# Router and latent projections: weights' high and low parts side by side in one moving operand

## The chip, the cores and the metric

The kernel runs on one core of a Trainium2 chip. The metric is the device time of one launch in microseconds (us). Before the change it is 628.88 us (median of three runs, 627.64 to 630.49). All inputs, weights and outputs are in float32 in HBM.

The engines are named as in the profile: PE is TensorE, PEld its loads of stationary operands, DVE VectorE, ACT ScalarE, POOL GpSimd and SP the engine that issues most DMAs.

## The reference

One transformer layer over 8 batches of 256 tokens of width 256: attention with compressed keys and values, then a mixture of experts. Only what the change touches is spelled out; rotary embedding, the routed experts and the shared expert are as usual.

```python
x = x + attention(layernorm(x))
#   kv = x_hat @ Wkv_a                     # [256 tokens, 64 latents + 64 rotary], per batch
#   kv_c = layernorm(kv[:, :64]) * gamma + beta;   k_rope = rope(kv[:, 64:])
#   k, v from kv_c @ Wkv_b;  16 heads of softmax(q k^T) v, then @ Wout
x = x + moe(layernorm(x))
#   logits = x_hat @ gate_w                # [256 tokens, 8 experts], per batch
#   scores = softmax(logits); the two best experts of each token, weighted by their scores
#   plus a shared expert for all tokens
```

## The kernel before

**Three products for one.** PE multiplies in the type float32r, which keeps fewer bits than float32. So each operand is kept as a high part (rounded) and a low part (what is left), and a product is the sum of three: high times high, high times low, low times high. The helper `three` (L222) issues them into one PSUM accumulation. Each is a load of a stationary operand and a matmul that streams the moving one.

**The two stages that change.** Each batch has two tiles j of 128 tokens and two halves k of the width.
- The latents, `prep_kv` (L250, PE): the normalised input `xa` is stationary, `Wkv_a` (`wkva_hi`, `wkva_lo`, 128 columns each) moves. Two tiles, two halves, three products: twelve matmuls of 128 columns. VectorE then takes mean and variance of the 64 latents from PSUM (`prep_kv`, DVE), the rotary products (`prep_rot`) and, a round later, the normalised latents (`prep_kn`), all from PSUM.
- The logits, `logits(b)` (PE): `xf` is stationary, `gate_w` (`gw_hi`, `gw_lo`, 8 columns) moves: again twelve matmuls. VectorE takes the maximum (`gate_max`, L1484), ScalarE the exponentials (`gate_exp`, L1288), both from PSUM.

**The order of the work.** All five engines run lists written out by hand, with semaphores between them. Attention is 64 rounds g, one for each pair of heads: i = g // 8 is the batch, r = g % 8 the round in it. In every round PE does two heads' scores (`ps_s`), four turns of probabilities (`ps_t<-ident,probs`), a query product (`ps_q`, twelve matmuls for pair g + 4), the turn of the norms (`ps_o<-ident,rinv`), the output projection (`ps_y`) and the products with the values (`ps_o`). Beside it the lists have work for other batches:
- at r = 2 and 3 the turn and the latents of batch i + 1; at r = 4 and 5 VectorE's and GpSimd's work on them
- at r = 6 and 7 the turn and the logits of batch i - 1 (from PE's first half of the round, ahead of the query product); at r = 0 and 1 of the next batch VectorE's masks and PE's ranks
- at r = 6 and 7 of batches 0 to 4 (and at 6 of batch 5) the split of one part of the expert weights: ScalarE makes its high part (`mgu_hi`, L469), VectorE the low one (`mgu_lo`, L477)

The last batch's logits stand behind attention, between products of the shared expert. Batch 6's come in round 62.

**The query buffer.** `ps_q` is one buffer. Of each query product ScalarE copies two pieces (`swap`, `qswap<-ps_q`), VectorE then multiplies it by the cosines (`query_cos`, `qf<-ps_q,qcos`, L1434, first in its list of the next round), and PE's next query product waits for that.

In round r = 7 ScalarE's list reads: copy of the norms (`norm<-ps_o`), high part of the weights, `gate_exp`, `swap`. VectorE's reads: low parts of the probabilities, low part of the weights, `gate_max`, the second maximum of the scores, and in the next round `query_cos`:

```python
if g in part_round: split_lo(part_round[g])          # DVE, order in a round
...
if routed(i, r) == 7 and batch(i - 1): gate_max(i - 1)
```

The front (until 50 us) makes the combined head weights, and holds the latents of batch 0; its 16 heads have lists of their own.

## Time and profile before

| what | us |
|---|---|
| median of three runs | 628.88 |
| the profiled execution, its own time | 629.82 |
| its span | 628.1 |
| PE busy | 605.3 |
| DVE busy | 467.8 |
| ACT busy | 475.0 |
| POOL busy | 410.2 |

PE is busy for 96% of the span. Its matmuls are pipelined: one lasts about 0.28 us, and the next starts 0.11 or 0.12 us behind it, so a busy PE need not be at its peak, and the length of a stage is read from the starts of its first matmul and of the first behind it. A row of a timeline begins with the start in us from the span's start and the length in us; in brackets stands the idle time before it and who ended it. The names read output<-inputs, for a matmul output<-moving,stationary.

### The profile page before, as it was taken

To read this page: it belongs to the slowest core of one execution; us is meant where nothing else is said; L and a number is where in the kernel's file an instruction comes from. 1 tells how busy PE (TensorE), PEld (TensorE's weight loads), DVE (VectorE), ACT (ScalarE), POOL (GpSimd) and SP (SyncE) were. 2 spreads that over 40 slices of the span, in tenths; PEclk is the share of its full clock that TensorE was granted. 3 is DMA by queue.
4 is the path that set the end of the run, shared out by engine and by line. 5 is a ranking of instruction groups with operands and counts; after the bars stand their busy time and mean duration, and the time that the engine had idled before them with its cause. 6 is when DMAs were issued, how large, how long until landed. Compare 5 with 4: busy or idle time off the path is not lost. (4 is left out here: it accounts for less than half of the span.)

```text
span 628.1 us, 15730 instructions
## 1 busy us (share of the span) xinstructions
PE 605.3 (96%) x4916; PEld 591.3 (94%) x4916; DVE 467.8 (74%) x1406; ACT 475.0 (76%) x1331; POOL 410.2 (65%) x455
## 2 busy tenths in 40 slices
PE   8998999999999999999999999999979989999995
PEld 8888999999999999999999999999978979999994
DVE  6667786877886878788688887778666676666486
ACT  4779999898988989889898898979864335556531
POOL 1467897786897889789789978978613204444400
PEclk9998999999999999999999999999999889999998
DMA  9792000000001001000100100020603155444292
GB/s 259 238 345 41 2 1 3 2 1 35 11 10 43 11 18 43 10 19 3 43 18 10 43 9 19 9 78 11 184 2 118 51 173 166 124 132 120 86 320 83
DMA packets 34024, 45.41 MB, mean 72 GB/s; under 512 B 4056, under 2 KB 29112, under 8 KB 33944
## 3 DMA queue, kind: packets, MB, share of 16 engines
q1 hardware_dynamic: 29160, 34.56, 17.6%
q0 software_dynamic: 3408, 9.34, 4.6%
q8 instruction: 42, 0.69, 0.5%
q10 hardware_dynamic: 1376, 0.50, 0.3%
q14 instruction: 38, 0.31, 0.2%
HBM read 27.57 MB, written 16.82 MB: 71 GB/s over the span
## 5 line engine op out<-in xcount | busy, mean ns | idle before, releaser
L1245 ACT ACTIVATE probs<-ps_s,nmax 128x256 f32<-128x256 f32 x256 | 119.1, 477 | 10.8 <-DVE nmax L1439 10.7
L1785 POOL TENSOR_TENSOR qswap<-qswap,qsin 128x512 f32<-128x512 f32 x64 | 83.3, 1301 | 43.6 <-ACT qswap L1222 43.6
L226 PE MATMUL ps_q<-xa,wq_hi 128*128 128x256 f32 x512 | 101.0, 295 | 3.7 <-DVE qf L1434 3.7
L1439 DVE TENSOR_REDUCE nmax<-ps_s 128x2 f32<-128x512 f32 x128 | 86.8, 678 | 9.3 <-PE ps_s L226 8.6
L1222 ACT ACTIVATE pT_hi<-ps_t 128x512 fp32r<-128x512 f32 x128 | 76.7, 599 | 17.0 <-PE ps_t L978 15.6
L1788 POOL TENSOR_TENSOR qf<-qf,qswap 128x512 f32<-128x512 f32 x64 | 82.7, 1292 | 10.5 <-DVE qf L1434 6.5
L1792 POOL TENSOR_TENSOR q_lo<-qf,q_hi 128x512 fp32r<-128x512 f32 x64 | 82.9, 1296 | 5.8 <-ACT q_hi L1222 5.8
L226 PEld LDWEIGHTS ps_q<-xa,wq_hi 128*128 128x128 f32 x512 | 79.9, 192 | 5.5 <-DVE qf L1434 3.3
L299 DVE TENSOR_TENSOR pT_lo<-ps_t,pT_hi 128x512 fp32r<-128x512 f32 x128 | 81.9, 681 | 1.5 <-ACT pT_hi L1222 1.5
L226 PE MATMUL ps_o<-pT_hi,kv_hi 128*128 128x256 f32 x256 | 76.7, 300 | 2.5 <-ACT norm L1222 2.5
L226 PE MATMUL ps_s<-kT_hi,q_hi 128*128 128x256 f32 x256 | 77.6, 303 | 0.9 <-ACT probs L1245 0.9
L978 PE MATMUL ps_t<-ident,probs 128*128 128x128 f32 x512 | 76.8, 273 | 1.3 <-DVE pT_lo L299 1.3
L1222 ACT ACTIVATE qswap<-ps_q 32x512 f32<-32x512 f32 x128 | 75.6, 590 | 3.3 <-PE ps_q L226 1.0
L1813 POOL DMA_INDIRECT routed_out<-yb,to x39 | 37.4, 959 | 57.7 <-DVE to L1574 55.1
L226 PE MATMUL ps_q<-xa,wq_lo 128*128 128x256 f32 x256 | 73.0, 285 | 0.0
L226 PE MATMUL ps_s<-kT_hi,q_lo 128*128 128x256 f32 x256 | 71.9, 281 | 0.0
L226 PE MATMUL ps_s<-kT_lo,q_hi 128*128 128x256 f32 x256 | 71.8, 280 | 0.0
L226 PE MATMUL ps_o<-pT_hi,kv_lo 128*128 128x256 f32 x256 | 71.5, 279 | 0.0
L226 PE MATMUL ps_o<-pT_lo,kv_hi 128*128 128x256 f32 x256 | 71.4, 279 | 0.0
L978 PEld LDWEIGHTS ps_t<-ident,probs 128*128 128x128 f32 x512 | 59.4, 141 | 1.7 <-issue 1.7
L1796 POOL TENSOR_TENSOR o_lo<-on,o_hi 128x256 fp32r<-128x256 f32 x64 | 47.3, 739 | 17.9 <-ACT o_hi L1222 17.5
L1434 DVE TENSOR_TENSOR qf<-ps_q,qcos 128x512 f32<-128x512 f32 x64 | 43.7, 683 | 15.8 <-ACT qswap L1222 15.6
(337 smaller groups left out, 1914.5 us busy)
## 6 DMA issues: line engine op xcount, KB each, us to landing
xg<-routed_in SPq DMA_DIRECT2D x39, 129.0 KB, 2.2
normal_turned<-xf SPq DMA_DIRECT2D x8, 512.0 KB, 2.8
wq_raw<-Wq_dram SPq DMA_DIRECT2D x16, 192.0 KB, 4.5
x<-x_dram SPq DMA_DIRECT2D x8, 256.0 KB, 5.7
xa<-normal_turned SPq DMA_DIRECT2D x4, 512.0 KB, 5.5
mgu_hi<-routed_out SPq DMA_DIRECT2D x4, 512.0 KB, 5.2
mgu_lo<-routed_out SPq DMA_DIRECT2D x4, 512.0 KB, 7.9
out_dram<-x SPq DMA_DIRECT2D x8, 256.0 KB, 2.9
```

What stands on the lines that cost most here:

```text
L226: last = nc.tensor.matmul(out, stat, mov, start=start and n == 0, stop=stop and n == len(terms) - 1, skip_group_check=skip)
L299: return vec.tensor_tensor(lo, src, hi.bitcast(F32), ALU.subtract)
L978: last = nc.tensor.transpose(turned[h % 2][:, c, tile(j)], probs[h % 3][:, j, tile(c)], L.ident[:, :])
L1222: copy = lambda out, src: nc.scalar.activation(out, src, ACT.Copy)
L1245: last = nc.scalar.activation(probs[h % 3][:, j, :], L.ps_s[h % 2][:, j, :], ACT.Exp, bias=nmax[:, h % NH, j:j + 1], accum_out=rsum[:, h % ...
L1434: vec.tensor_tensor(qf[g % 2][:, :, :], L.ps_q[:, :, :], L.qcos[:, :].unsqueeze(1).to_broadcast([P, 2, S]), ALU.mult).then_inc(ev.qcos_don ...
L1439: vec.tensor_reduce(nmax[:, h % NH, :], L.ps_s[h % 2][:, :, :], AX.X, ALU.max, negate=True).then_inc(ev.max_done, 1)
L1785: gp.tensor_tensor(qs, qs, L.qsin[:, :].unsqueeze(1).to_broadcast([P, 2, S]), ALU.mult).then_inc(ev.qrot_part, 1)
L1788: gp.tensor_tensor(to, to, qs, ALU.add).then_inc(ev.qrot_done, 1)
L1792: gp.tensor_tensor(q_lo[g % 2][:, :, :], qf[g % 2][:, :, :], q_hi[g % 2][:, :, :].bitcast(F32), ALU.subtract).then_inc(ev.qlo_done, 1)
L1796: gp.tensor_tensor(o_lo[g % 2][:, :], on[g % 2][:, :], o_hi[g % 2][:, :].bitcast(F32), ALU.subtract).then_inc(ev.olo_done, 1)
L1813: gp.indirect_dma_start(ys[:, :], bass.IndirectOffsetOnAxis(to[:, j:j + 1], 0), yb[j % 3][:, :], None).then_inc(ev.y_stored[j % 3], 16)
```

## The change

The high and the low part of `Wkv_a` lie side by side (`wkva`, 2 x 128 columns for each half of the width), and so do those of `gate_w` (`gw`, 2 x 8). The stationary high part of the input meets both in one matmul, and the stationary low part too. That makes 2 (halves) x 2 (parts of the input) matmuls for a tile and eight for a stage, in place of twelve; the product of the two low parts, which was left out before, is now in the sum. PSUM then holds two groups of columns for a tile. VectorE adds them in one reduction each: into `L.kv` (two tiles of 128 columns, which lie in `xhat_a`), and into `L.logit`. What read PSUM before now reads these two.

`xhat_a` gets a second use, so ScalarE's next normalisation (`prep_normal`) waits for the rotary products and the normalised latents, and VectorE's addition waits for those of the batch before.

```diff
@@ class Layer
-        self.wkva_hi, self.wkva_lo = (sb(f"wkva_{x}", [P, KD, RANK + DR], F32R) for x in ("hi", "lo"))
-        self.gw_hi, self.gw_lo = (sb(f"gw_{x}", [P, KD, E], F32R) for x in ("hi", "lo"))
+        self.wkva = sb("wkva", [P, KD, 2, RANK + DR], F32R)
+        self.wkva_hi, self.wkva_lo = (self.wkva[:, :, n, :] for n in range(2))
+        self.gw = sb("gw", [P, KD, 2, E], F32R)
+        self.gw_hi, self.gw_lo = (self.gw[:, :, n, :] for n in range(2))
+        self.logit = sb("logit", [P, NT, E])
...
+        self.kv = self.xhat_a[:, 0, :].rearrange("p (j n) -> p j n", j=NT)
@@ PE, prep_kv
-            last = three(L.kv_spot(b)[:, tile(j)],
-                         [(xa_hi[:, k, tile(j)], xa_lo[:, k, tile(j)], L.wkva_hi[:, k, :], L.wkva_lo[:, k, :])
-                          for k in range(KD)])
+            parts = [x[:, k, tile(j)] for k in range(KD) for x in (xa_hi, xa_lo)]
+            for n, x in enumerate(parts):
+                last = nc.tensor.matmul(L.kv_spot(b)[:, j, :], x, L.wkva[:, n // 2, :, :].rearrange("p n c -> p (n c)"),
+                                        start=n == 0, stop=n == len(parts) - 1)
@@ ACT, prep_normal
-            act.wait_ge(ev.xa_turned, b)
+            act.wait_ge(ev.kr_done, b)
+            act.wait_ge(ev.kn_done, b)
@@ DVE, prep_kv
-        moments(lambda j: L.kv_spot(b)[:, j * P:j * P + RANK], L.mean_k, L.var_k, ev.vark_done)
+            dve.wait_ge(ev.kr_done, b)
+            dve.wait_ge(ev.kn_done, b)
+        step(vec.tensor_reduce(L.kv[:, :, :], L.kv_spot(b)[:, :, :].rearrange("p j (n c) -> p j c n", n=2), AX.X, ALU.add))
+        moments(lambda j: L.kv[:, j, 0:RANK], L.mean_k, L.var_k, ev.vark_done)
@@ DVE, prep_rot (prep_kn likewise)
-        rot = L.kv_spot(b).rearrange("p (j n) -> p j n", j=NT)
+        rot = L.kv
@@ PE, logits
-                    last = three(misc[:, 0, j * E:(j + 1) * E],
-                                 [(xf_hi[:, k, tile(j)], xf_lo[:, k, tile(j)], L.gw_hi[:, k, :], L.gw_lo[:, k, :]) for k in range(KD)])
+                    parts = [x[:, k, tile(j)] for k in range(KD) for x in (xf_hi, xf_lo)]
+                    for n, x in enumerate(parts):
+                        last = nc.tensor.matmul(misc[:, 0, j * 2 * E:(j + 1) * 2 * E], x, L.gw[:, n // 2, :, :].rearrange("p n e -> p (n e)"),
+                                                start=n == 0, stop=n == len(parts) - 1)
@@ ACT, gate_exp
-                    last = nc.scalar.activation(eprob[:, j, :], misc[:, 0, j * E:(j + 1) * E], ACT.Exp,
+                    last = nc.scalar.activation(eprob[:, j, :], L.logit[:, j, :], ACT.Exp,
@@ DVE, gate_max
-                vec.tensor_reduce(lmax[:, :], misc[:, 0, 0:NT * E].rearrange("p (j e) -> p j e", j=NT), AX.X, ALU.max,
-                                  negate=True).then_inc(ev.lmax_done, 1)
+                if b >= 1:
+                    dve.wait_ge(ev.gate_exp_done, b)
+                step(vec.tensor_reduce(L.logit[:, :, :], misc[:, 0, 0:2 * NT * E].rearrange("p (j n e) -> p j e n", j=NT, n=2), AX.X, ALU.add))
+                vec.tensor_reduce(lmax[:, :], L.logit[:, :, :], AX.X, ALU.max, negate=True).then_inc(ev.lmax_done, 1)
```

`step` lets VectorE wait until the instruction it wraps has ended. Three places show how the lists change. First VectorE's list around the latents in round r = 3 (before):

```order
L299 TENSOR_TENSOR pT_lo<-ps_t,pT_hi 128x512 x2
L311 BN_STATS bn<-ps_m 128x6 x2
L307 MEMSET carrier 128x1
L314 BN_AGGR mean_k<-bn 128x2 x2
L316 TENSOR_SCALAR mean_k<-mean_k 128x2
L317 TENSOR_SCALAR var_k<-mean_k 128x2
L1439 TENSOR_REDUCE nmax<-ps_s 128x2
L1434 TENSOR_TENSOR qf<-ps_q,qcos 128x512
```

The same place in the changed kernel (its line numbers are its own; `xhat_a` is where `L.kv` lies):

```order
L309 TENSOR_TENSOR pT_lo<-ps_t,pT_hi 128x512 x2
L353 TENSOR_REDUCE xhat_a<-ps_m 128x256
L321 BN_STATS bn<-xhat_a 128x6 x2
L317 MEMSET carrier 128x1
L324 BN_AGGR mean_k<-bn 128x2 x2
L326 TENSOR_SCALAR mean_k<-mean_k 128x2
L327 TENSOR_SCALAR var_k<-mean_k 128x2
L1454 TENSOR_REDUCE nmax<-ps_s 128x2
L1449 TENSOR_TENSOR qf<-ps_q,qcos 128x512
```

One reduction of 512 elements to 256 is new, ahead of the maximum of the scores and of `qf`, for which PE's query product waits. Next VectorE's list from the end of round r = 7 into the next, around the logits (before):

```order
L299 TENSOR_TENSOR pT_lo<-ps_t,pT_hi 128x512 x2
L477 TENSOR_TENSOR mgu_lo<-mgu_raw,mgu_hi 128x4x176
L1484 TENSOR_REDUCE lmax<-ps_m 128x2
L1439 TENSOR_REDUCE nmax<-ps_s 128x2
L1434 TENSOR_TENSOR qf<-ps_q,qcos 128x512
```

And in the changed kernel:

```order
L309 TENSOR_TENSOR pT_lo<-ps_t,pT_hi 128x512 x2
L489 TENSOR_TENSOR mgu_lo<-mgu_raw,mgu_hi 128x4x176
L1501 TENSOR_REDUCE logit<-ps_m 128x16
L1502 TENSOR_REDUCE lmax<-logit 128x2
L1454 TENSOR_REDUCE nmax<-ps_s 128x2
L1449 TENSOR_TENSOR qf<-ps_q,qcos 128x512
```

A small reduction stands between the low part of the weights and the maximum of the logits. Last, PE's list in the changed kernel at the latents, which stand between the turned probabilities and the query product as before:

```order
L233 MATMUL ps_s<-kT_hi,q_lo 128x256
L990 MATMUL ps_t<-ident,probs 128x128 x4
L264 MATMUL ps_m<-wkva,xa 128x256 x8
L233 MATMUL ps_q<-xa,wq_hi 128x256 x2
L233 MATMUL ps_q<-xa,wq_lo 128x256
```

Where eight matmuls of 256 columns stand, there were twelve of 128. At the logits eight of 16 columns stand in the place of twelve of 8.

## Rows read from the trace of the kernel before

**Rows 1.** The page, part 1: busy time of TensorE, VectorE and ScalarE.
```profile
PE 605.3 (96%) x4916; PEld 591.3 (94%) x4916; DVE 467.8 (74%) x1406; ACT 475.0 (76%) x1331; POOL 410.2 (65%) x455
```

**Rows 2.** Busy times by stretch: us; PE, PEld, DVE, ACT, POOL; clock; DMA share; GB/s.
```profile
165.55:172.96 7.41, 7.41 (x66) 7.41 (x65) 5.47 (x13) 6.05 (x18) 6.12 (x7) 1.00 0.08 22
172.96:179.02 6.06, 6.06 (x54) 6.06 (x53) 4.99 (x20) 4.83 (x13) 5.76 (x8) 1.00 0.07 23
191.80:199.21 7.41, 7.41 (x66) 7.41 (x65) 5.39 (x11) 6.61 (x19) 7.14 (x9) 1.00 0.24 91
199.21:205.88 6.67, 6.33 (x55) 6.09 (x54) 3.35 (x8) 5.15 (x15) 3.69 (x4) 1.00 0.00 0
205.88:212.83 6.95, 6.78 (x59) 6.69 (x58) 6.57 (x29) 6.63 (x19) 6.25 (x7) 1.00 0.08 24
...
360.48:366.54 6.06, 6.06 (x54) 6.06 (x53) 3.64 (x8) 5.33 (x17) 4.90 (x5) 1.00 0.01 3
```

**Rows 3.** Timeline of PE: start, us, instruction; round 19's latents, round 23's logits, 256-wide products.
```profile
170.11 0.31 PE L226 MATMUL ps_m<-wkva_hi,xa 128*128 128x128 f32 x1
...
171.48 0.45 PE L226 MATMUL ps_q<-xa,wq_hi 128*128 128x256 f32 x2
...
196.36 0.25 PE L226 MATMUL ps_m<-gw_hi,xf 128*128 128x8 f32 x1
...
197.70 0.48 PE L226 MATMUL ps_q<-xa,wq_hi 128*128 128x256 f32 x2
...
201.39 0.28 PE L226 MATMUL ps_o<-pT_lo,kv_hi 128*128 128x256 f32 x1
...
202.57 0.28 PE L226 MATMUL ps_o<-pT_hi,kv_lo 128*128 128x256 f32 x1
```

**Rows 4.** Timelines of ACT, DVE and PE, rounds 23 and 24, by time.
```profile
199.63 0.39 ACT L1222 ACTIVATE norm<-ps_o 128x256 f32<-128x256 f32 x1 [0.89 <-PE ps_o L1004]
199.91 0.78 ACT L469 ACTIVATE mgu_hi<-mgu_raw 128x704 fp32r<-128x704 f32 x1
200.72 0.89 DVE L477 TENSOR_TENSOR mgu_lo<-mgu_raw,mgu_hi 128x704 fp32r<-128x704 f32 x1 [1.90 <-ACT mgu_hi L469]
201.53 0.17 DVE L1484 TENSOR_REDUCE lmax<-ps_m 128x2 f32<-128x16 f32 x1
201.74 0.27 ACT L1288 ACTIVATE eprob<-ps_m,lmax 128x8 f32<-128x8 f32 x1 [1.04 <-DVE lmax L1484]
...
203.59 0.69 DVE L1434 TENSOR_TENSOR qf<-ps_q,qcos 128x512 f32<-128x512 f32 x1 [1.29 <-ACT qswap L1222]
...
204.34 0.51 PE L226 MATMUL ps_q<-xa,wq_hi 128*128 128x256 f32 x2 [0.34 <-DVE qf L1434]
```

**Rows 5.** Timeline of ACT, round 15: the copy of the norms.
```profile
145.87 0.39 ACT L1222 ACTIVATE norm<-ps_o 128x256 f32<-128x256 f32 x1 [0.16 <-PE ps_o L1004]
```

**Rows 6.** Timelines of DVE and PE, round 28: rotation's first product, next query.
```profile
228.97 0.68 DVE L1434 TENSOR_TENSOR qf<-ps_q,qcos 128x512 f32<-128x512 f32 x1
...
231.28 0.48 PE L226 MATMUL ps_q<-xa,wq_hi 128*128 128x256 f32 x2
```

**Rows 7.** Groups by line: VectorE's reduction of 512 PSUM elements.
```profile
L1439 DVE TENSOR_REDUCE nmax<-ps_s 128x2 f32<-128x512 f32 x128 | 86.8, 678 | 9.3 <-PE ps_s L226 8.6
```

**Rows 8.** Timeline of DVE: a small reduction and what waits for its end.
```profile
161.01 0.19 DVE L1516 TENSOR_REDUCE row_f<-choice 128x4 f32<-128x32 f32 x1
161.23 0.17 DVE L1517 CAST slots<-row_f 128x4 int32<-128x4 f32 x1
```

**Rows 9.** Timeline of DVE in the front: head 6's first low part.
```profile
25.99 0.29 DVE L707 TENSOR_TENSOR wq_lo<-ps_o,wq_hi 128x128 fp32r<-128x128 f32 x1 [0.77 <-ACT wo_hi L583]
```

**Rows 10.** Timelines of ACT and DVE at the end of attention and behind.
```profile
459.52 0.27 ACT L1288 ACTIVATE eprob<-ps_m,lmax 128x8 f32<-128x8 f32 x1 [1.44 <-DVE lmax L1484]
...
494.00 0.17 DVE L1510 TENSOR_TENSOR where<-ps_m,base 128x16 f32<-128x16 f32 x1 [3.88 <-PE ps_m L1040]
```

**Rows 11.** Busy times of a stretch behind attention; clock is the sixth number.
```profile
480.00:490.00 10.00, 8.82 (x57) 8.41 (x56) 6.73 (x33) 6.63 (x15) 4.32 (x5) 0.78 0.30 109
```

More of the change, by code:

```diff
@@ L214, in kv_spot @@
     def kv_spot(self, b):
-        return (self.ps_s[1] if b == 0 else self.ps_m)[:, 0, :]
+        return self.ps_s[1] if b == 0 else self.ps_m
     def k_spot(self, b):
@@ L340, in prep_kv @@
             dve.wait_ge(ev.rsk_done, b)
-        moments(lambda j: L.kv_spot(b)[:, j * P:j * P + RANK], L.mean_k, L.var_k, ev.vark_done)
+            dve.wait_ge(ev.kr_done, b)
+            dve.wait_ge(ev.kn_done, b)
+        step(vec.tensor_reduce(L.kv[:, :, :], L.kv_spot(b)[:, :, :].rearrange("p j (n c) -> p j c n", n=2), AX.X, ALU.add))
+        moments(lambda j: L.kv[:, j, 0:RANK], L.mean_k, L.var_k, ev.vark_done)
     def prep_rot(b):
-        dve.wait_ge(ev.kv_full, b + 1)
         if b >= 1:
             dve.wait_ge(ev.kp_done, b)
-        rot = L.kv_spot(b).rearrange("p (j n) -> p j n", j=NT)
+        rot = L.kv
         evens, odds = rot[:, :, RANK::2], rot[:, :, RANK + 1::2]
@@ L358, in prep_kn @@
         for j in range(NT):
-            last = vec.tensor_scalar(kp[:, j, 0:RANK], L.kv_spot(b)[:, j * P:j * P + RANK], L.rstd_k[:, j:j + 1], L.off_k[:, j:j + 1],
+            last = vec.tensor_scalar(kp[:, j, 0:RANK], L.kv[:, j, 0:RANK], L.rstd_k[:, j:j + 1], L.off_k[:, j:j + 1],
                                      ALU.mult, ALU.add)
@@ L568, in small @@
         act.wait_ge(F.small_in, 32)
-        nc.scalar.activation(L.wkva_hi[:, :, :], F.small_raw[:, :, 0:RANK + DR], ACT.Copy).then_inc(F.small_hi, 1)
-        nc.scalar.activation(L.gw_hi[:, :, :], F.small_raw[:, :, RANK + DR:], ACT.Copy).then_inc(F.small_hi, 1)
+        nc.scalar.activation(L.wkva_hi, F.small_raw[:, :, 0:RANK + DR], ACT.Copy).then_inc(F.small_hi, 1)
+        nc.scalar.activation(L.gw_hi, F.small_raw[:, :, RANK + DR:], ACT.Copy).then_inc(F.small_hi, 1)
         act.dma_start(L.gamma[:, :], d["gamma"].partition_broadcast(P)).then_inc(F.scales_in, 16)
@@ L689, in small @@
         dve.wait_ge(F.small_hi, 2)
-        vec.tensor_tensor(L.wkva_lo[:, :, :], F.small_raw[:, :, 0:RANK + DR], L.wkva_hi[:, :, :].bitcast(F32), ALU.subtract)
-        vec.tensor_tensor(L.gw_lo[:, :, :], F.small_raw[:, :, RANK + DR:], L.gw_hi[:, :, :].bitcast(F32), ALU.subtract)
+        vec.tensor_tensor(L.wkva_lo, F.small_raw[:, :, 0:RANK + DR], L.wkva_hi.bitcast(F32), ALU.subtract)
+        vec.tensor_tensor(L.gw_lo, F.small_raw[:, :, RANK + DR:], L.gw_hi.bitcast(F32), ALU.subtract)
     def trig():
```

## Prediction

> **What bounds the kernel now.** The page's busy times come first: PE 605.3 of 628.1 us, the others 65 to 76% [rows 1]. That alone doesn't say that PE sets the pace, so I cut attention at the starts of PE's turns of the norms, once a round, and read the stretches' lengths. A round with nothing extra takes 6.06 us, and the one with the latents or the logits in its first half 7.41 (the stretch from 172.96 against those from 165.55 and 191.80) [rows 2]. These lengths repeat to 0.01 us over the batches, and PE is busy for all of each: there PE's list is the time. The exceptions are the two stretches behind a round 7 that holds both the logits and a split of weights. The first, with nothing extra on PE, takes 6.67 in place of 6.06; the same stretch of batch 6, with no split ahead, takes 6.06 (from 199.21 and from 360.48) [rows 2]. PE waits there for `qf`, and the timelines show for what chain: norms copied, high part of the weights, low part, `lmax`, `eprob`, the copies of `ps_q`, `qf`, and PE's query at 204.34 [rows 4]. So the question is which of the saved PE time lies in stretches that PE owns, and what the two additions do to this chain.
>
> **The latents.** The twelve products of 128 columns take 170.11 to 171.48, 1.37 us, and the round is 1.35 longer than a plain one: 0.1125 each [rows 3, 2]. Products of 256 columns start 1.18 us apart over ten steps, 0.118 each (201.39 to 202.57) [rows 3]. Eight of them are 0.94 us, so a stage saves 1.35 - 0.94 = 0.41 us. That twice the columns cost nearly the same has its reason in the next stage: products of 8 columns take 196.36 to 197.70, again 0.112 each [rows 3], so below 256 columns the number of products sets the price.
>
> A rule of the Trainium skill speaks against that. "TensorE: Matmul & The Clock Gate", section "Back-to-back issue gap", gives the gap of an isolated warm matmul as N/2.4 + 2.5 ns, 56 ns for 128 columns and 109 for 256. By it a stage of the latents would grow from 0.67 to 0.87 us. The trace doesn't agree for these products, each with a stationary operand of its own: it has 112 ns at 128 columns, as the section's own remark, that in a real stream the loads count too, lets one expect.
>
> VectorE pays for it with a reduction of 512 PSUM elements. The nearest row is the maximum over 512 elements from PSUM, 0.68 us [rows 7]; the new one reads pairs 128 elements apart and writes 256. I take 0.68, and 0.04 for the wait on its end (a small reduction of 0.19 holds the next instruction for 0.22) [rows 8]. Bounds: 0.4, since what follows now reads SBUF, and four times the row, 2.7, if the stride costs that much. It lands in stretches where VectorE is busy 5.47 of 7.41 us and 4.99 of 6.06 [rows 2]. What is queued behind it is a maximum of scores and `qf`, for which PE's next query waits. That `qf` ends at 228.97 + 0.68 = 229.65, the query starts at 231.28: 1.63 us to spare [rows 6]. PE comes 0.41 earlier and `qf` 0.72 later, which leaves 0.50. GpSimd's powers start later too; its list is nearly full there (5.76 of 6.06 us) but empty enough some rounds on (3.69 of 6.67) [rows 2], and I take it to catch up. So the addition costs nothing in these seven batches (1 to 7, made in batches 0 to 6): 7 x 0.41 = 2.87 us saved. If that cover were gone, each would cost what exceeds 1.22 us.
>
> The latents of batch 0 lie in the front, where loads and other engines pace PE. VectorE's next work there waits 0.77 us for ScalarE [rows 9], which takes the 0.72. I count 0; bounds are 0.41 gained and 0.7 lost.
>
> **The logits.** Eight products at 0.1125 are 0.90 us, so PE has 0.45 less a stage. VectorE's addition of 32 elements costs 0.22 by the small reduction's row [rows 8]; bounds 0.1 and 0.35 (ScalarE's two exponentials now read SBUF, which the trace has not for this size). Stage by stage:
> - Batches 1 to 3 (rounds 23, 31, 39): the chain begins at PE's norms, behind the logits: ScalarE had waited 0.89 us for them [rows 4]. So all of the 0.45 passes into it. But the addition lies inside the chain, since `eprob` waits 1.04 us for `lmax` [rows 4]: + 0.22. Net 0.23 each, 0.69. The second late stretch (205.88, with the ranks) hangs on the same chain through the exponentials and masks, so the 0.22 is paid once, not twice.
> - Batch 0 (round 15): ScalarE waits only 0.16 for the norms [rows 5], so the chain starts at most 0.16 earlier, and the other 0.29 comes back as PE's wait for `qf`. With the addition: 0.06 lost.
> - Batches 4 and 5 (rounds 47, 55) have no split in the round. The chain is shorter by the high and the low part, 0.78 + 0.89, and where it was 0.61 late it has about 1.1 to spare [rows 2, 4]. Full gain, 0.90.
> - Batch 6 (round 62): queries are over, PE has less to do, and ScalarE and VectorE hand each other the work; `eprob` waits 1.44 us for `lmax` [rows 10]. Nothing gained, 0.22 lost.
> - Batch 7 (behind attention): VectorE has waited 3.88 us for PE's ranks [rows 10], so PE's list is the time up to there and the addition is hidden: 0.45 gained.
>
> Sum of the logits: 0.69 - 0.06 + 0.90 - 0.22 + 0.45 = 1.76 us.
>
> **The other edits** I cost at nothing. The rotary products and the normalised latents read SBUF in place of PSUM, in a list with idle time. ScalarE's normalisation at r = 0 waits for `kn_done`, which is some three rounds old. The split of the small weights is the same work with another stride, in the front. The product of the low parts takes no instruction of its own.
>
> **The sum.** 2.87 + 1.76 = 4.6 us. The profiled execution took 629.82 us (span 628.1), 0.94 above the median; its span should come to 623.5. Set against the median: 628.88 - 4.6 = 624.3 us.
>
> **The rivals.**
> - *The wait moves.* VectorE's and ScalarE's lists, with 0.72 us more, become the bound around the latents, and the 2.87 comes back as waits for `qf` or for low parts. For it: VectorE's 5.47 us in that stretch become 6.2 of 7.00, and PE already waits in two stretches a batch [rows 2]. Against: the spare 1.63 us [rows 6]. Time: 628.9 - 1.8 = 627.1. Chance 0.14.
> - *The saving comes in full.* The additions hide and every logits stage gives 0.45: 7 x 0.41 + 8 x 0.45 = 6.5, 622.4 us. Against: `eprob` waits for `lmax` in rounds 15 to 39 and 62. Chance 0.07.
> - *Columns set the price.* At 0.118 for 256 columns, 128 would take 0.059: a stage of latents grows from 0.71 to 0.94, seven lose 1.6 us, the logits gain nothing and their additions cost 1.1: 631.6 us. This is what the cited gap would do here. Against: 0.112 at 128 and at 8 columns alike [rows 3]. Chance 0.03.
> - *The clock moves.* Behind attention the granted clock falls to its lower level: 0.78 on average over 480 to 490 us [rows 11], at full speed but for 4.4 us at 1.2 in place of 2.4 GHz. That costs 2.2 us of PE's time in these ten. The same event missing, or one more, gives about 622.1 or 626.5. Chance 0.10, half on either side.
> - *Slower: the strided addition.* The reduction of pairs 128 elements apart takes not 0.68 but 2.7 us, and stands ahead of `qf` seven times. It hurts from 1.22 us on (1.63 spare less 0.41). Price: 7 x (2.7 - 1.22) = 10.4 us, less the 4.6: 634.6. It makes the kernel slower by over 0.5% from 2.3 us on. For it: no row shows such a read. Against: VectorE's other strided reads in this kernel show nothing of the kind. Chance 0.06.
>
> **How the numbers follow.** A measurement of this kernel tells about 0.5% (3.1 us) from no change, that is 625.7 and 632.0. The forecast has 0.60, with 622.0 to 626.0 as its own range. Below 625.7 lie 0.55 of it, the full saving and half of the clock's: 0.66 or so. Within 0.5%: the rest of the forecast 0.05, the moved wait 0.14, the columns 0.03, half of the clock's 0.05: 0.28. Slower: 0.06. The range 621.5 to 627.8 takes in the forecast, the moved wait, the full saving and most of the clock's, and leaves out columns and stride.
>
> **What would show it.** In the changed profile: rounds with latents 7.00 us and those with logits 6.96, at eight products of 0.118 and 0.112; the addition 0.68 us, and 0.5 us between the next `qf` and its query. The stretch behind rounds 23, 31 and 39 should take 6.67 + 0.22 = 6.89, behind round 15 about 7.2, and behind 47 and 55 still 6.06. The forecast is wrong if products of 16 columns take another time than those of 8, if the addition exceeds 1.2 us, or if plain rounds are no longer 6.06.

## The result, and the profile after

The changed kernel takes 626.57 us (median of 8 runs, 624.10 to 627.67), the kernel before in the same session 629.11 (8 runs, 627.64 to 630.49). The ratio is 0.9949, with 95% interval 0.9927 to 0.9970. So it is faster, by 2.5 us in place of 4.6. Run again later on another chip it gave 0.9917 (0.9887 to 0.9947), with 10 runs of it and 15 of before.

The page of the changed kernel, busy times and the group of PE's query products:

```profile
PE 597.2 (96%) x4852; PEld 582.6 (93%) x4852; DVE 490.8 (78%) x1422; ACT 474.9 (76%) x1331; POOL 411.1 (66%) x455
...
L233 PE MATMUL ps_q<-xa,wq_hi 128*128 128x256 f32 x512 | 99.6, 292 | 6.8 <-DVE qf L1449 6.6
```

The same group of the kernel before:

```profile
L226 PE MATMUL ps_q<-xa,wq_hi 128*128 128x256 f32 x512 | 101.0, 295 | 3.7 <-DVE qf L1434 3.7
```

Against [rows 1] PE has 64 matmuls and 8.1 us less work, VectorE 16 instructions and 23.0 us more. The 16 additions are 5.5 + 1.5 = 7.0 us of it. Most of the other 16 is not work, as is shown below. The last number of the group says where part of PE's saving went: it waits 6.6 us for `qf`, where it waited 3.7.

Cut at the starts of PE's turns of the norms as before, the stretches of the changed kernel are (length; PE, PEld, DVE, ACT, POOL; clock; DMA share; GB/s):

```profile
163.59:170.57 6.98, 6.98 (x62) 6.98 (x61) 5.10 (x11) 6.03 (x18) 5.88 (x6) 1.00 0.07 22
170.57:176.63 6.06, 6.06 (x54) 6.06 (x53) 5.71 (x23) 4.75 (x13) 4.92 (x9) 1.00 0.07 23
189.38:196.32 6.94, 6.94 (x62) 6.94 (x61) 5.82 (x12) 6.88 (x20) 6.51 (x9) 1.00 0.25 97
196.32:203.71 7.39, 6.32 (x54) 6.08 (x53) 4.39 (x10) 5.53 (x17) 5.60 (x5) 1.00 0.00 0
203.71:210.65 6.94, 6.77 (x59) 6.68 (x58) 6.55 (x30) 6.62 (x19) 6.25 (x7) 1.00 0.07 24
257.25:265.32 8.07, 7.04 (x60) 6.72 (x58) 7.69 (x30) 6.61 (x19) 6.20 (x7) 1.00 0.05 16
```

The rounds with the latents or the logits are 0.42 and 0.47 shorter, PE is busy for all of them, and a plain round is still about 6.06, all as against [rows 2]. The loss is in the late stretches. Behind rounds 23, 31 and 39 the first takes 7.39, 7.38 and 7.38, where it took 6.67 and 6.89 was forecast. The second takes 6.94, 8.07 and 8.08, where it took 6.93 to 6.95 and was to stay.

Round 23 and 24 of the changed kernel, timelines of GpSimd, ScalarE, VectorE and PE by time, the answer to [rows 4]:

```profile
196.74 0.38 ACT L1237 ACTIVATE norm<-ps_o 128x256 f32<-128x256 f32 x1
197.02 0.79 ACT L481 ACTIVATE mgu_hi<-mgu_raw 128x704 fp32r<-128x704 f32 x1
197.14 1.29 POOL L1809 TENSOR_TENSOR q_lo<-qf,q_hi 128x512 fp32r<-128x512 f32 x1
197.84 1.34 DVE L489 TENSOR_TENSOR mgu_lo<-mgu_raw,mgu_hi 128x704 fp32r<-128x704 f32 x1 [1.10 <-ACT mgu_hi L481]
198.38 1.39 POOL L1813 TENSOR_TENSOR o_lo<-on,o_hi 128x256 fp32r<-128x256 f32 x1
199.10 0.18 DVE L1501 TENSOR_REDUCE logit<-ps_m 128x16 f32<-128x32 f32 x1
199.31 0.17 DVE L1502 TENSOR_REDUCE lmax<-logit 128x2 f32<-128x16 f32 x1
199.52 0.30 ACT L1303 ACTIVATE eprob<-logit,lmax 128x8 f32<-128x8 f32 x1 [1.71 <-DVE lmax L1502]
...
201.44 0.69 DVE L1449 TENSOR_TENSOR qf<-ps_q,qcos 128x512 f32<-128x512 f32 x1 [1.36 <-ACT qswap L1237]
...
202.19 0.50 PE L233 MATMUL ps_q<-xa,wq_hi 128*128 128x256 f32 x2 [1.07 <-DVE qf L1449]
```

The chain is the one that was forecast, with the addition in it. But the low part of the weights takes 1.34 us in place of 0.89. GpSimd's `q_lo` is in flight when it starts and ends at 198.43; `mgu_lo` ends 0.75 behind that. Then GpSimd's next, `o_lo`, is held in turn, 1.39 in place of its usual 0.74. So two instructions that touch no common data hold each other up.

In the kernel before, GpSimd's part of that moment looks like this (timeline of GpSimd):

```profile
198.73 1.29 POOL L1792 TENSOR_TENSOR q_lo<-qf,q_hi 128x512 fp32r<-128x512 f32 x1
199.99 0.74 POOL L1796 TENSOR_TENSOR o_lo<-on,o_hi 128x256 fp32r<-128x256 f32 x1
```

`o_lo` ends at 200.73, and `mgu_lo` began at 200.72 [rows 4]. The two were clear of each other by nothing. Measured from PE's turn of the norms, `q_lo` started 0.48 us ahead of it before (199.21) and starts 0.82 behind it now (196.32), while `mgu_lo` starts 1.51 and 1.52 behind it: GpSimd came 1.30 us later into a place where VectorE didn't.

The second collision is at the masks. Timelines of VectorE, GpSimd and PE behind round 31 of the changed kernel, in the stretch of 8.07 us:

```profile
261.24 1.27 POOL L1802 TENSOR_TENSOR qswap<-qswap,qsin 128x512 f32<-128x512 f32 x1 [0.29 <-ACT qswap L1237]
261.24 1.30 DVE L1521 TENSOR_TENSOR choice<-both,choice 128x16 f32<-128x16 f32 x1
262.60 0.27 PE L1055 MATMUL ps_m<-both,before 128*128 128x8 f32 x1 [0.55 <-DVE choice L1521]
...
263.80 0.50 PE L233 MATMUL ps_q<-xa,wq_hi 128*128 128x256 f32 x2 [0.48 <-DVE qf L1449]
```

The last mask has 16 elements and takes 0.17 us elsewhere. Here it takes 1.30 and ends 0.03 behind GpSimd's rotation, which started in the same hundredth. PE waits for the mask and then once more for `qf`; the stretch is 1.13 us longer than the same one of batch 1 (203.71).

The Trainium skill has a rule for this, which I had not weighed: "SBUF — State Buffer", section "SBUF: two separate sides". VectorE and GpSimd share a pair of ports; a VectorE instruction in a two-port mode and a GpSimd instruction exclude each other, and so do a VectorE instruction with two SBUF inputs and a GpSimd instruction that reads SBUF; whoever starts first keeps the ports to its end, and the other is blocked whole. The trace agrees: 0.89 becomes 1.34 and 0.17 becomes 1.30.

Waits of this kind are not new. The kernel before has them at other places, and the change moves them, one to the good. In round 14 VectorE makes `sd_lo`, the low part of another weight. Timelines of GpSimd and VectorE before, and then in a version with the latents' half of the change alone (`e_lat`, below):

```profile
139.62 0.73 POOL L1796 TENSOR_TENSOR o_lo<-on,o_hi 128x256 fp32r<-128x256 f32 x1
139.70 1.20 DVE L477 TENSOR_TENSOR sd_lo<-sd_raw,sd_hi 128x512 fp32r<-128x512 f32 x1 [1.55 <-ACT sd_hi L469]
```

```profile
138.77 0.69 DVE L487 TENSOR_TENSOR sd_lo<-sd_raw,sd_hi 128x512 fp32r<-128x512 f32 x1 [1.03 <-ACT sd_hi L479]
139.48 0.92 POOL L1807 TENSOR_TENSOR o_lo<-on,o_hi 128x256 fp32r<-128x256 f32 x1
```

GpSimd comes later there too, VectorE has its 0.69 us undisturbed, and GpSimd waits a little instead. It is 0.69 in the changed kernel as well, and 1.25 with the logits' half alone.

A third place is of the change's own making. The rotary products of the keys read the latents from SBUF where they read PSUM before. Groups by line of the kernel before, and then of the changed one:

```profile
L350 DVE TENSOR_TENSOR krot<-ps_m,kcos 128x64 f32<-128x64 f32 x14 | 3.0, 214 | 0.0
L350 DVE TENSOR_TENSOR krot<-ps_m,ksin 128x64 f32<-128x64 f32 x14 | 2.4, 214 | 0.0
```

```profile
L362 DVE TENSOR_TENSOR krot<-xhat_a,ksin 128x64 f32<-128x64 f32 x16 | 9.4, 628 | 0.0
L362 DVE TENSOR_TENSOR krot<-xhat_a,kcos 128x64 f32<-128x64 f32 x16 | 6.6, 412 | 0.0
```

With 0.4 and 0.3 us for the same products of batch 0, which lie in `ps_s`, 6.1 us have become 16.0, though a product by itself still takes 0.21: the means of 0.63 and 0.41 hold waits for GpSimd (in each of batches 2 to 7 one product of 1.32 and one of 0.59; that of 231.37 ends 0.08 behind GpSimd's `q_lo`). That is 9.9 us of VectorE's growth. PE has no product that waits for it. But it uses up cover in rounds r = 4, and GpSimd's work on the keys waits for these products (0.43 us at 233.04).

### The profile page after: what moved, and what is told of

It is laid out like the page before. It is cut to its first block and busy times, and to the rows that moved or that the text cites. A ratio compares the mean times of both kernels' runs of the same rounds, so it can differ in the third digit from the quotient of the medians.

```text
span 625.2 us, 15625 instructions
## 1 busy us (share of the span) xinstructions
PE 597.2 (96%) x4852; PEld 582.6 (93%) x4852; DVE 490.8 (78%) x1422; ACT 474.9 (76%) x1331; POOL 411.1 (66%) x455
## 5 line engine op out<-in xcount | busy, mean ns | idle before, releaser
L233 PE MATMUL ps_q<-xa,wq_hi 128*128 128x256 f32 x512 | 99.6, 292 | 6.8 <-DVE qf L1449 6.6
L1813 POOL TENSOR_TENSOR o_lo<-on,o_hi 128x256 fp32r<-128x256 f32 x64 | 49.4, 772 | 18.1 <-ACT o_hi L1237 17.8
L1260 ACT ACTIVATION_READ_ACCUMULATOR probs<-ps_s,nmax 128x1 f32 x256 | 53.0, 207 | 0.0
```

The lines of the kernel that those rows point to most:

```text
L233: last = nc.tensor.matmul(out, stat, mov, start=start and n == 0, stop=stop and n == len(terms) - 1, skip_group_check=skip)
L1260: last = nc.scalar.activation(probs[h % 3][:, j, :], L.ps_s[h % 2][:, j, :], ACT.Exp, bias=nmax[:, h % NH, j:j + 1], accum_out=rsum[:, h % ...
L1813: gp.tensor_tensor(o_lo[g % 2][:, :], on[g % 2][:, :], o_hi[g % 2][:, :].bitcast(F32), ALU.subtract).then_inc(ev.olo_done, 1)
```

## The experiments

Lengths of stretches are from one profiled execution each. "Attention" is from the first turn of the norms to the last. It leaves out the front and the end, which differ between profiles of one kernel: the changed kernel had its first turn at 54.89 and 55.73, and 159.7 and 157.1 us from the last one to the end, with granted clocks of 0.94 and 0.98 over 460 to 540 us.

| kernel | ratio to before (95%) | first late stretch behind 23, 31, 39 | second | attention |
|---|---|---|---|---|
| before | 1 | 6.67 6.67 6.67 | 6.95 6.93 6.93 | 411.61 |
| changed | 0.9949 (0.9927, 0.9970) | 7.39 7.38 7.38 | 6.94 8.07 8.08 | 410.65 |
| changed, again | 0.9917 (0.9887, 0.9947) | 7.37 7.37 7.34 | 8.02 8.08 6.91 | 410.13 |
| latents alone | 1.0002 (0.9979, 1.0025) | 7.24 7.23 7.20 | 6.94 6.95 6.95 | 410.88 |
| logits alone | 0.9979 (0.9956, 1.0002) | 7.28 7.28 7.28 | 6.95 6.95 6.95 | 410.70 |
| before, low part moved | 0.9954 (0.9931, 0.9977) | 6.06 6.05 6.06 | 7.56 7.56 6.62 | 409.83 |
| changed, low part moved | 0.9824 (0.9799, 0.9849) | 6.04 6.05 6.05 | 6.62 6.61 6.61 | 402.92 |
| no addition of logits | one run, 626.52 us | 7.08 7.04 7.07 | 8.09 8.08 8.07 | 409.85 |
| addition of latents twice | 0.9995 (0.9962, 1.0029) | 7.50 7.48 7.46 | 8.07 8.08 8.07 | 415.30 |
| GpSimd's `q_lo` behind `mgu_lo` | 0.9912 (0.9880, 0.9943) | 6.93 6.95 6.95 | 6.95 6.88 6.96 | 406.85 |
| GpSimd's rotation behind masks | 0.9933 (0.9902, 0.9963) | 7.36 7.62 7.32 | 6.95 6.95 7.00 | 409.06 |
| both waits | 0.9858 (0.9818, 0.9898) | 6.94 6.95 6.94 | 6.95 6.90 6.89 | 406.64 |
| low part moved, rotation behind masks | 0.9877 (0.9832, 0.9922) | 6.05 6.05 6.05 | 6.61 6.61 6.61 | 401.62 |

### The two halves apart

`e_lat` keeps the logits of before and has only the latents side by side; `e_log` the other way round. In `e_lat`, where the changed kernel has one moving operand of 16 columns:

```diff
-    last = nc.tensor.matmul(misc[:, 0, j*2*E:(j+1)*2*E], x, L.gw[:, n//2, :, :]..., ...)
+    last = three(misc[:, 0, j*E:(j+1)*E], [(xf_hi..., xf_lo..., L.gw_hi..., L.gw_lo...) for k in range(KD)])
-    step(vec.tensor_reduce(L.logit[:, :, :], misc[...]..., AX.X, ALU.add))
```

> The latents' half of the change alone, logits as before. Theory (each stage of latents pays in full, VectorE's addition is covered): the seven rounds with latents 6.99 us in place of 7.41, the stretches behind rounds 15 to 39 as before, 6.67 and 6.94; median 629.1 - 2.9 = 626.2. Rival (the addition moves the wait to the query of the next rounds): those rounds grow over 6.06 and 6.28, and the median stays at 628 or above.

> The logits' half alone, latents as before. Theory (PE saves 0.47 in each of six rounds 7, but in four of them VectorE's low part of the weights now starts while GpSimd still holds the SBUF port that both need, and waits for it): rounds 7 take 6.94 us, the stretch behind round 15 about 6.95, behind 23, 31 and 39 about 7.38; the second stretch 6.94, or 8.08 where VectorE's last mask loses the port to GpSimd's rotation. Median 628 to 629. Rival (the addition of logits alone is what costs, 0.22 in the chain): 6.89 behind 23, 31 and 39, median 627.3.

Measured: 628.67 us (12 runs) and 627.26 (12), against 628.69 (26 runs). Neither theory came out: the latents alone were to give 2.9 us and gave nothing, and the logits alone, with first late stretches of 7.28 where 7.38 was expected and no mask lost, came to the time of their rival (627.3) without its stretches (6.89). Each half shortens its own rounds about as forecast (7.41 to 7.04, 7.41 to 6.94), and each alone lengthens the first late stretch to 7.2 or 7.3. The latents' half, which has no part in the chain, does that too. Timelines of `e_lat`, GpSimd and VectorE:

```profile
197.91 1.30 POOL L1803 TENSOR_TENSOR q_lo<-qf,q_hi 128x512 fp32r<-128x512 f32 x1
199.16 0.74 POOL L1807 TENSOR_TENSOR o_lo<-on,o_hi 128x256 fp32r<-128x256 f32 x1
199.19 1.46 DVE L487 TENSOR_TENSOR mgu_lo<-mgu_raw,mgu_hi 128x704 fp32r<-128x704 f32 x1 [1.64 <-ACT mgu_hi L479]
```

and of `e_log`:

```profile
199.09 1.29 POOL L1798 TENSOR_TENSOR q_lo<-qf,q_hi 128x512 fp32r<-128x512 f32 x1
200.33 0.74 POOL L1802 TENSOR_TENSOR o_lo<-on,o_hi 128x256 fp32r<-128x256 f32 x1
200.59 1.23 DVE L479 TENSOR_TENSOR mgu_lo<-mgu_raw,mgu_hi 128x704 fp32r<-128x704 f32 x1 [1.43 <-ACT mgu_hi L471]
```

PE's turns of the norms are at 197.67 and 199.08 here, so `q_lo` starts 0.24 and 0.01 behind them, against 0.48 ahead in the kernel before. Against PE's turn the latents' half makes GpSimd 0.72 us later, the logits' half 0.49 (there the turn comes 0.47 earlier, and GpSimd stays where it was), both together 1.30. The chain of the kernel before could take none of it. What in the latents' half makes the 0.72, the addition or the longer rotary products, these runs don't tell apart.

### The low part moved out of the chain

VectorE's split of the weights goes behind the maxima of the logits in the rounds r = 7, in the changed kernel and, the same way, in the one before:

```diff
-    if g in part_round:
+    late = g in part_round and r == 7
+    if g in part_round and not late:
         split_lo(part_round[g])
 ...  # gate_max
+    if late:
+        split_lo(part_round[g])
```

> The changed kernel, with VectorE's low part of the weights moved behind the maximum of the logits in rounds 7. Theory (the chain norms, high part, low part, addition, maximum, exponentials, swap, qf is what swallows the logits' gain): without the low part in it the stretches behind rounds 15 to 39 are 6.06 us, the second ones 6.6 to 6.7, or up to 7.8 where the last mask still meets GpSimd's rotation; 4.9 us less from the first and about 1.3 from the second, median 619 to 621. Rival (ScalarE's own list is the bound there, not the low part): the first stretches stay over 6.5, median above 624.

> The kernel before, with the same move. Theory: its four late stretches of 6.67 us become 6.06 and the second ones 6.62, 3.8 us less: 625.3. So the change by itself, with the chain out of the way (this kernel against the changed one with the same move), is worth 5 to 6.5 us. Rival (ScalarE's own list): less than 1 us.

Measured: 618.82 us (5 runs) and 626.83 (9). With the chain out of the way the changed kernel is 8.0 us faster than its counterpart, on one chip, and 9.9 faster than before, the lowest ratio of this study. Timelines of `e_order_after`, GpSimd and VectorE:

```profile
194.74 0.17 DVE L1502 TENSOR_REDUCE lmax<-logit 128x2 f32<-128x16 f32 x1
194.99 1.30 POOL L1812 TENSOR_TENSOR q_lo<-qf,q_hi 128x512 fp32r<-128x512 f32 x1
195.71 1.32 DVE L489 TENSOR_TENSOR mgu_lo<-mgu_raw,mgu_hi 128x704 fp32r<-128x704 f32 x1 [0.80 <-ACT mgu_hi L481]
```

The collision is still there, 1.32 us, but nobody on PE's way waits for it: the first late stretch is 6.05, a plain round. In the kernel before the move makes room too (6.67 to 6.06), and two of its masks then lose the race against the rotation (1.33 us, stretches of 7.56 against 6.62), which takes back 1.9 of what it gave. The difference of 8.0 holds those 1.9; in attention it is 6.9. Against that stands one stretch of 7.47 for 6.48 in the changed kernel's profile. Without either the change is worth 6.0 us in attention once the chain is out of the way, inside the 5 to 6.5 expected, while the time of 625.3 expected for the kernel before with the move was missed by 1.5.

### The additions alone

`e_noadd` leaves the addition of the logits out, and with it the low part of `gate_w`: the maximum and the exponentials read the first 8 of the 16 columns. `e_add2` makes the addition of the latents twice.

```diff
 # e_noadd
-    step(vec.tensor_reduce(L.logit[:, :, :], misc[...]..., AX.X, ALU.add))
-    vec.tensor_reduce(lmax[:, :], L.logit[:, :, :], AX.X, ALU.max, negate=True)
+    vec.tensor_reduce(lmax[:, :], misc[...]...[:, :, 0, :], AX.X, ALU.max, negate=True)
 # e_add2
     step(vec.tensor_reduce(L.kv[:, :, :], L.kv_spot(b)[:, :, :]..., AX.X, ALU.add))
+    step(vec.tensor_reduce(L.kv[:, :, :], L.kv_spot(b)[:, :, :]..., AX.X, ALU.add))
```

> The changed kernel without VectorE's addition of the logits: the low part of gate_w is left out of them, the maximum and the exponentials read the high group in PSUM. Theory (the addition is 0.22 us in the chain of four stretches, on top of the wait for the port): 6.7 behind round 15, 7.15 behind 23, 31 and 39. Rival (the port's wait hides it): 7.38 as with it.

> The changed kernel with VectorE's addition of the latents done twice. Theory (0.51 us to spare before the query of round r = 4 and 0.33 before that of r = 5, by the changed kernel's profile): another 0.7 us eats that and PE waits 0.2 at r = 4 and some at r = 5, in seven batches: 1.4 to 3 us more, median 628 to 629.5. Rival (VectorE catches up, cover as forecast before the change): no wait, 626.6. Both hold the addition itself for 0.68 us.

Without the addition the first late stretch is 7.04 to 7.08, 0.31 to 0.34 less, the one behind round 15 6.65 in place of 6.95, and the last three of attention 18.98 in place of 19.27; the collision of `mgu_lo` stays (1.32). So the addition costs 0.3 in the chain and not 0.22: 0.21 to the maximum, and the rest in ScalarE's two exponentials, which read SBUF (timeline of ScalarE in `e_noadd`):

```profile
199.38 0.27 ACT L1303 ACTIVATE eprob<-ps_m,lmax 128x8 f32<-128x8 f32 x1 [1.47 <-DVE lmax L1500]
...
199.63 0.26 ACT L1303 ACTIVATE eprob<-ps_m,lmax 128x8 f32<-128x8 f32 x1
```

They start 0.25 apart from PSUM, and 0.30 from SBUF in the changed kernel (199.52 and 199.82).

The addition of the latents: timeline of VectorE in `e_add2`, and PE's next query.

```profile
170.14 0.68 DVE L353 TENSOR_REDUCE xhat_a<-ps_m 128x256 f32<-128x512 f32 x1
170.86 0.69 DVE L354 TENSOR_REDUCE xhat_a<-ps_m 128x256 f32<-128x512 f32 x1
...
174.21 0.68 DVE L1450 TENSOR_TENSOR qf<-ps_q,qcos 128x512 f32<-128x512 f32 x1
...
175.04 0.47 PE L233 MATMUL ps_q<-xa,wq_hi 128*128 128x256 f32 x2
```

0.68 us, 0.72 from start to start, with pairs 128 elements apart: the plain maximum's time [rows 7] to the hundredth. The second one is no longer free. `qf` ends 0.15 ahead of the query, and the rounds r = 4 and 5 are 0.31 and 0.28 longer (6.37 for 6.06, 6.55 for 6.27), about 0.6 a batch. One addition fits into the cover, two don't. The time, 630.10 us (10 runs) against 629.69 (21), is a little over the 628 to 629.5 expected, and its profile also lost all three races at the masks.

### Taking the collisions away

GpSimd takes the low part of the queries only when VectorE has the low part of the weights (`e_lo_first`), or rotates only behind the masks (`e_masks_first`), or both (`e_lo_masks2`). No instruction is added or left out.

```diff
+    if r == 1 and batch(i - 2):                           # masks
+        pool.wait_ge(ev.masks_done, i - 1)
     if pair(g + 3):
         rotate(g + 3)
+    if g in part_round and r == 7 and i >= 2:             # low part
+        pool.wait_ge(ev.part_lo, splits_upto(L, part_round[g]))
     if pair(g + 2):
         query_lo(g + 2)
```

> The changed kernel; in rounds 23, 31 and 39 GpSimd waits for VectorE's low part of the weights before it starts q_lo, so that the two cannot meet. Theory (VectorE's instruction with two SBUF inputs waits for GpSimd's running one): mgu_lo takes 0.89 us in place of 1.33, and the stretches behind these rounds fall from 7.38 to about 6.94, although GpSimd works later. Rival (mgu_lo is long for another reason, or the chain starts elsewhere): mgu_lo stays over 1.2 us and the stretches at 7.38. Median about 625.3, less clear than the stretches.

> The changed kernel; at r = 1 GpSimd waits for the masks before it starts the next rotation. Theory (where the last mask and the rotation start together, either can have the port, and VectorE then waits 1.13 us): the last mask takes 0.17 to 0.18 us everywhere, the second late stretches 6.94 in all four batches, and the times bunch around the lower group of the changed kernel's, 624.3. Rival (the two groups of times come from the clock or the loads): still two groups, median 626.6.

Measured: 624.63 us (6 runs) and 625.71 (8), against 629.69 (21). The first brings `mgu_lo` back to 0.89 and the three stretches to 6.93 to 6.95, the 6.89 of the forecast but for the dearer exponentials. It also won all three races at the masks, which it was not made for. The second brings the mask to 0.18 and the second stretches to 6.95 to 7.00, and leaves the first ones. Its time was to be 624.3 and is not: its profile has a new wait of the same kind in round 28 (a stretch of 7.47, shown at the end) and a first late stretch of 7.62 behind it.

> Both waits of GpSimd at once, of the changed kernel: GpSimd takes the low part of the queries only behind VectorE's low part of the weights in rounds 23, 31 and 39, and rotates only behind the masks one round on. Theory (the lost gain is VectorE's instructions that wait while GpSimd's runs): mgu_lo 0.89 us and the last mask 0.17 in all of batches 1 to 3, so that both late stretches of each are 6.93 to 6.96, six in all, against 7.38 three times, 6.94 once and 8.07 twice in the changed kernel. That is 3 x 0.44 + 2 x 1.13 = 3.6 us less than its profile in a repeated execution: 0.986 to 0.991 of before. Rival (GpSimd, held back, becomes late itself and PE's query waits for its low parts): the masks' 0.17 come, but the stretches stay over 7.2 or grow elsewhere, and the time is that of the changed kernel, ratio 0.993 to 0.997. Medians on two chips don't compare to better than 1 us.

In this kernel the wait for the low part stood one step too early, before the rotation in place of behind it. It took 630.30 us (12 runs), 1.0027 of before (1.0001 to 1.0052), with stretches of 9.04, 9.99 and 10.45: GpSimd idled 4.28 us, and PE's scores then waited for it.

```profile
200.62 0.39 PE L233 MATMUL ps_s<-kT_hi,q_hi 128*128 128x256 f32 x1 [2.73 <-POOL q_lo L1809]
```

It says nothing on the question, but it shows how little GpSimd can be held back. With the wait in its place:

> As e_lo_masks was meant: GpSimd waits for VectorE's low part of the weights directly before its low part of the queries (in e_lo_masks the wait stood one step too early, before the rotation, so that PE waited 2.73 us for GpSimd's q_lo and the first late stretches took 9.0 to 10.5), and for the masks before it rotates one round on. Theory of the collisions: mgu_lo 0.89 and the last mask 0.18 in batches 1 to 3, first and second late stretches 6.93 to 7.00, six in all, 3.4 to 3.8 us less than a profile of the changed kernel; ratio to before 0.986 to 0.992, and 0.991 to 0.997 of the changed kernel beside it. Rival (holding GpSimd back costs what it gives): first stretches over 7.2, ratio 0.993 to 0.998 to before and 0.998 to 1.003 to the changed kernel.

> The changed kernel again, on the chip of e_lo_masks2, so that the two can be set side by side: 0.993 to 0.997 of before. Its late stretches should be as in its first profile where the waits are fixed by the order (7.38 behind rounds 23, 31 and 39), while those that hang on the race at the last mask may come out at 6.94 or 8.07 in any batch. Rival (the collisions are an accident of one execution): first late stretches other than 7.38, between 6.9 and 7.5 by chance.

Measured on one chip: 622.33 us (6 runs) with both waits, 625.60 (10) without, 630.89 (15) before. The waits give 3.3 us. Timelines of `e_lo_masks2`, VectorE and GpSimd:

```profile
195.72 0.89 DVE L489 TENSOR_TENSOR mgu_lo<-mgu_raw,mgu_hi 128x704 fp32r<-128x704 f32 x1 [1.14 <-ACT mgu_hi L481]
196.53 0.18 DVE L1501 TENSOR_REDUCE logit<-ps_m 128x16 f32<-128x32 f32 x1
196.70 1.29 POOL L1809 TENSOR_TENSOR q_lo<-qf,q_hi 128x512 fp32r<-128x512 f32 x1 [1.70 <-DVE mgu_lo L489]
```

The repeat of the changed kernel has `mgu_lo` at 1.32, 1.32 and 1.30: that collision is set by the order. The race at the masks isn't fixed so: it fell to GpSimd in batches 1 and 2 here, in 2 and 3 the first time. Behind round 39 both started at 317.43 and VectorE won (timelines of the repeat):

```profile
317.43 0.18 DVE L1521 TENSOR_TENSOR choice<-both,choice 128x16 f32<-128x16 f32 x1
317.43 1.33 POOL L1802 TENSOR_TENSOR qswap<-qswap,qsin 128x512 f32<-128x512 f32 x1 [0.30 <-ACT qswap L1237]
```

This race isn't new either. Timelines of VectorE and GpSimd in the kernel before, batch 1:

```profile
209.86 0.17 DVE L1504 TENSOR_TENSOR choice<-both,choice 128x16 f32<-128x16 f32 x1
209.86 1.31 POOL L1785 TENSOR_TENSOR qswap<-qswap,qsin 128x512 f32<-128x512 f32 x1 [0.31 <-ACT qswap L1222]
```

Over batches 1 to 3 VectorE lost none of twelve in the profiles of the kernel before, of either half alone and of `e_lo_first`, ten of twelve in the two of the changed kernel, `e_noadd` and `e_add2`, and two of three in `e_order_before`. The two starts lie within 0.03 us of each other in all of them. So the change seems to have shifted them by some 0.02 us to the bad side, and the wait in `e_lo_first` to have undone it; by what way isn't shown.

### Low part moved and masks first

> The changed kernel with VectorE's low part of the weights behind the maxima of the logits in rounds 23, 31, 39 and 15, and GpSimd's rotation behind the masks. Theory: with the low part moved the first late stretch is 6.05 and the second 6.61 in the profile of the version that had the move alone, so there is nothing left for the masks' wait to take away, except in executions where the race at the last mask is lost: 617.5 to 620.5, ratio 0.980 to 0.985. Rival (the waits of GpSimd cost its list, which is nearly full in the rounds behind): 620 to 624, with longer stretches in rounds 24 to 30.

619.70 us (6 runs, 617.39 to 625.82), inside the 617.5 to 620.5 expected, and 0.9877 of before (0.9832 to 0.9922), for 0.980 to 0.985, span 617.5 as with the move alone. No collision is left on PE's way and attention is 401.62, 1.30 less than with the move alone, 1.0 of it one stretch of 7.47 for 6.48 that the latter's profile had (of the kind shown at the end). Whether it beats the move alone in time stays open: the two ran on different chips and their intervals overlap.

## Why the prediction was right in direction and 2 us too good

The direction is right. The time of 626.57 lies outside the forecast's own 622.0 to 626.0, where the rival of the moved wait had its 627.1; only the wide range, which was drawn to take that rival in, holds it. Point by point:

- **Products: right.** The products of 256 columns start 0.118 apart, those of 16 columns 0.112, as those of 8 and 128 did; rounds with latents are 0.42 shorter (0.41 forecast), those with logits 0.47 (0.45). The rival that columns set the price is refuted. But the 0.41 hit is in part chance: the eight products take 1.03 us and not 0.94 (168.13 to 169.16, with 0.20 from the first to the second), and the latents' half alone makes its rounds 0.37 shorter.
- **The latents: right up to PE's next query.** The addition takes 0.68, `qf` is 0.51 ahead of the query (0.50 forecast from [rows 6]). The six stages of batches 2 to 7 give 6 x 0.42. That of batch 1 gave 0.36 and 0.68 in the two profiles. What failed is the sentence on GpSimd, "I take it to catch up". From PE's turn, its `q_lo` is later than before by 1.08 us in round 20 of `e_lat`, 1.59 in 21, 1.02 in 22 and still 0.72 in 23, and level again only in 24. So the latents cost time elsewhere, in the logits' chain. `e_lat` shows it: seven stages give some 2.6 (7 x 0.37), three first late stretches take back 1.66.
- **Batches 4 and 5: right.** 0.47 each, and 6.05 behind them. A third, small loss of 0.09 behind round 56 wasn't forecast.
- **Round 15: too dark, and better by luck.** 0.19 gained (14.08 to 13.89 us over two stretches), 0.06 lost by forecast. With the logits' half alone the forecast is met to the hundredth: ScalarE copies the norms 0.65 behind PE's turn (145.98 behind 145.33), where it was 0.42 before (145.87 behind 145.45 [rows 5]), and the two stretches take 14.14 (6.94 + 7.20), 0.06 lost. What makes it better is the latents' half. It takes away the wait of `sd_lo` one round earlier (1.20 to 0.69 us), VectorE's and ScalarE's lists run 0.28 ahead of where they were, in `e_lat` ScalarE then waits 0.44 for the norms in place of 0.16, and in the changed kernel its copy is at 0.42 again (143.64 behind 143.22).
- **Batches 1 to 3: the step that failed**, "all of the 0.45 passes into it ... Net 0.23 each". It did pass, and `mgu_lo`, 0.45 longer, ate it. The round with the logits and the stretch behind it took 14.08 us before (7.41 + 6.67), 13.88 in the version with both waits, so 0.20 is there to be had, and 14.33 in the changed kernel. The excess over 6.89 is 0.50 + 0.49 + 0.49 = 1.48 us (some 0.05 of each is the dearer exponentials). That the second late stretch "hangs on the same chain" and the cost is paid once failed as well: 1.13 + 1.15 = 2.28 more, by the race at the masks.
- **The end of attention: right.** 19.01 to 19.27 us in its last three stretches, 0.26 lost (0.22 forecast), and 18.98 without the addition.
- **The other edits, costed at nothing: wrong in kind.** "The rotary products and the normalised latents read SBUF in place of PSUM, in a list with idle time" is true, but it makes the rotary products wait for GpSimd, 9.9 us in all.
- **Batch 7 and the front** can't be told: both move by more from one profile to the next than the 0.45 and 0.4 in question. The rival of the clock bears on the end: the granted clock over 480 to 490 us was 0.78 before [rows 11], 0.83 and 1.00 in the two profiles of the changed kernel, and the end of the latter was 2.5 us shorter.

The account closes. For attention the forecast was 2.87 + 1.53 - 0.22 = 4.2 us. The profile gave 0.96; with 1.48 + 2.28 added it is 4.7, and the version with both waits measured 411.61 - 406.64 = 4.97. The 0.24 between them is one stretch, that behind round 56 (6.85 to 6.61), where a mask had lost to GpSimd's rotation in the kernel before too (1.15 us at 421.91, 0.17 with both waits). The rival "the wait moves" had the right size (627.1) and a wrong place: it spoke of full lists around the latents, and the loss is in two engines in each other's way four rounds on. A slip without weight: its chances below 625.7 add up to 0.67 and those within 0.5% to 0.27, where it has 0.66 and 0.28.

Which of the two parts is the larger in the time of an ordinary run stays open, since the race at the masks falls differently each time. That may be part of the spread of the changed kernel's runs; it wasn't shown.

## What to carry to other kernels

Before an edit that makes one engine later against another, lay the timelines of VectorE and GpSimd over each other and mark VectorE's instructions with two SBUF inputs and its TENSOR_SCALARs from SBUF to SBUF, those too that the edit itself turns from PSUM to SBUF: a gap of 0.01 us between one and the end of a GpSimd instruction is no spare but an edge. "It catches up" needs a row in which that engine idles before the next place that matters. Look for the waits that the kernel has already, instructions that take longer than others of their shape, since the edit can take one away as well as make one (round 15). And a stretch that a chain sets is worth more than the work in it: moving one instruction of 0.89 us behind the chain gave 1.9 us, the change 2.5, and both together 9.9.

## What the runs showed of the hardware

- A blocked VectorE instruction ends a fixed time behind GpSimd's: that time is its own length less some 0.14 us. `mgu_lo` (0.89 alone) ends 0.75 behind `o_lo` in `e_lat` (200.65 and 199.90) and `e_log` (201.82 and 201.07), 0.75 behind `q_lo` in the changed kernel, 0.74 in `e_order_after`. `sd_lo` (0.69) ends 0.55 behind `o_lo` in the kernel before, the mask (0.17) 0.03 behind. So a collision costs what is left of GpSimd's instruction, less 0.14.
- Started in the same hundredth of a microsecond, either side can win: 261.24 went to GpSimd, 317.43 to VectorE. In the trace's nanoseconds GpSimd had started 9 ahead in the first and 2 ahead in the second. The last mask and the rotation start within 0.06 us of each other 38 times in the profiles here: GpSimd won all 11 in which it was 9 ns or more ahead, VectorE all 25 in which it was ahead or at most 3 ns behind, and of the two at 6 ns each won one.
- It doesn't need two inputs. Tiny float32 instructions of one SBUF input waited too: timeline of VectorE in `e_masks_first`, the stretch of 7.47 us, with GpSimd's `q_lo` from 236.25 on. Whether this is the two-port mode of the Trainium skill's rule, no run here shows.

```profile
225.10 0.17 DVE L326 TENSOR_SCALAR mean_f<-mean_f 128x2 f32<-128x2 f32 x1
...
236.71 0.85 DVE L326 TENSOR_SCALAR mean_a<-mean_a 128x2 f32<-128x2 f32 x1
237.48 0.78 DVE L327 TENSOR_SCALAR var_a<-mean_a 128x2 f32<-128x2 f32 x1
```

- A reduction of 512 PSUM elements in pairs 128 apart, with 256 results, takes the 0.68 us of a plain maximum with two results.
